# Moving the one other stage of a step ahead of the values on TensorE, in an attention and feed-forward kernel

## The chip, the cores and the metric

The kernel runs on one core of a Trainium2 chip. The metric is the device time of one execution in microseconds (us). The median of three runs of the kernel before is 1005.7 us (1003.91 to 1006.5). TensorE, VectorE, ScalarE, GpSimd and SyncE are called PE, DVE, ACT, POOL and SP, as in the profile. All numbers of the computation are 32-bit floats.

## The reference, cut to what matters

Eight batches of 512 query rows and 1024 context rows, width 256, 16 heads of 16 columns. Each batch goes through cross-attention and then through a feed-forward part that works on 128 selected rows:

```python
x = x + xattn(layernorm(x), ctx, ctx, mask, w_q, w_k, w_v, w_o)
x = x + ffn(layernorm(x), w_router, W_qkv, W_out, g1, g2, W1, W2, W3)

def xattn(q, k, v, mask, ...):          # 16 heads of 16
    scores = (q @ w_q.T) . (k @ w_k.T) / sqrt(16)     # per head, 512 x 1024
    attention = softmax(where(mask, -1e9, scores))
    return (attention . (v @ w_v.T)) @ w_o.T

def ffn(x, ...):                         # 128 of 512 rows
    idx = top_k(x @ w_router, 128)
    x_sel = x[idx]
    h = rmsnorm(x_sel, g1)
    x_attn = causal_attention(h @ W_qkv.T) @ W_out.T
    h2 = rmsnorm(x_sel + x_attn, g2)
    x_ff = silu(h2 @ W1.T) * (h2 @ W2.T) @ W3.T
    out = x.at[idx].set(x_sel + x_attn + x_ff)
```

## The kernel before, in words

Each batch is worked in 32 steps: four groups of four heads, eight tiles of 128 keys in each. In step `s` PE computes the scores of step `s` (`pe_scores`, L412, four matmuls that each use 32 rows of the array) into two of three pairs of PSUM banks. ACT takes the exponential of each pair (`act_scores`, L449, line L454), and writes it to `probs`. PE multiplies `probs` of the step before with the values (`pe_values`, L429, line L443), and adds them up in `o_bank` over the eight steps of a group. So the order on PE is scores of step `s`, then values of step `s - 1`.

The softmax needs one more pass when a group is complete. The last values of a group (steps 7, 15, 23 and 31; PE issues them in the step after, so those of step 31 in step 0 of the next batch) release `o_ready`. `dve_norm` (L526) then transposes `o_bank`, takes reciprocals, multiplies, and after groups 1 and 3 transposes again. These are the stages `norm0` to `norm3` of DVE.

Everything else is cut into other stages, at most two in a step. Stages of kind P belong to the projections of the next batch (`K00` to `K11`, `V0` to `V3`, `xT0`, `xT1`, `Q0`, `Q1`; `pe_project`, L252). Stages of kind F belong to the feed-forward part of the batch before (`wo0` to `scat0`; `pe_ffn`, L285). In a step without such a stage only scores and values run; it is called a plain step here. All these stages write one PSUM bank, `m_bank`. PE takes it with `take_bank` (L247; L248 and L249 are a wait on `bank_free`), and the next stage can start only when ACT or DVE has read the result of the last one out and released the bank. The exception is `fs`, the scores of the small attention, which uses the pairs of the ring.

The order of the stages is written out by hand for each engine. `PE_SLOT` gives for PE the kind, the stage, its step, and a flag that is called `early` in the loop at L994. With `early` the stage is issued between the scores and the values of its step, without it behind the values. Batch 0 has its own table, `PE_SLOT_0`. Batch 7 has no stage of kind P. `ACT_SLOT` places the stages that ACT reads out, always after both exponentials of the step. `DVE_ORDER` is a list without steps: DVE takes its stages strictly one after the other and waits at each for its input. Part of that list, which matters for the order of work:

```python
("F", "rank0"), ("F", "rank1"), ("N", "norm0"), ("F", "rank2"), ("F", "rank3"), ("P", "xn"), ("F", "gather"),
...
("F", "wout"), ("P", "V3"), ("N", "norm2"), ("F", "u0"), ("F", "w0"), ("F", "u1"), ("F", "w1"), ("F", "down"),
```

Some stages of PE wait for more than the bank. `gather` waits for the selection matrix `sel` that DVE makes in `rank0` to `rank3`. `Q0` waits for both halves of `xn_t`, which ACT copies out after `xT0` and `xT1`. `u0` waits for `hid2_t`, which ACT copies out after `hid2T`. The bank of `u0` is released by DVE in stage `u0` (L692), which stands behind `norm2` in `DVE_ORDER`.

Of the kernel before, what the change touches and what calls it, by code (L numbers as in the profile page):

```python
# [5 lines left out]
P = 128  # L6
# [43 lines left out]


FS_STEP = 16
PE_SLOT = [("P", "K00", 0, False), ("P", "K01", 1, False), ("F", "wo0", 2, False), ("F", "wo1", 3, False),
           ("P", "V0", 4, True), ("P", "K10", 5, False), ("F", "spread", 6, False), ("P", "K11", 7, False),
           ("F", "gather", 10, False), ("F", "selT", 11, False), ("F", "hidT", 12, False), ("P", "V1", 13, True),
           ("P", "xT0", 13, False), ("F", "kq", 14, False), ("F", "v", 15, False), ("F", "fs", FS_STEP, False),
# [4 lines left out]
ACT_SLOT = [("P", "K00", 0), ("P", "K01", 1), ("P", "K10", 5), ("F", "spread", 6), ("P", "K11", 7), ("P", "differ", 9),  # L61
            ("F", "selT", 11), ("F", "hidT", 12), ("P", "xT0", 13), ("F", "v", 15), ("F", "fs", FS_STEP), ("P", "xT1", 16),
            ("F", "hid2T", 23), ("F", "u0", 24), ("F", "u1", 26)]
# [33 lines left out]
def program(nc, io, out):  # L97
    with ExitStack() as top:
# [669 lines left out]
        def slots(b, table):  # L768

            has = {"A": b > 0, "F": b > 0, "N": True, "P": b < B - 1, "I": True}  # L770
            return [e[1:] + (e[0],) for e in table if has[e[0]]]
# [5 lines left out]
        with ExitStack() as ctx:  # L777
# [191 lines left out]
            def _(pe):  # L969
# [20 lines left out]
                for b in range(B):  # L990
                    todo = slots(b, PE_SLOT if b > 0 else PE_SLOT_0)
                    if b == 1:
# [316 lines left out]
```

## Time and profile before

| | |
|---|---|
| median of three runs | 1005.7 us |
| profiled execution: time | 1004.58 us |
| its span, first to last instruction | 1002.9 us |
| granted TensorE clock, mean | 0.973 |
| PE busy | 909.9 us (91%) |
| ACT busy | 575.9 us (57%) |
| DVE busy | 340.6 us (34%) |
| POOL busy | 78.7 us (8%) |

A row of the timeline gives the start in us, the busy time of the merged instructions, the engine, the line, the operation, what it writes and reads, and the count. Behind it stands in brackets how long the engine was idle before it, and on what it waited; `PEq` and `DVEq` are the sequencers of PE and DVE, and L422 and L249 lines in the semaphore handling of the scores and of `take_bank`. Every matmul of 32-bit floats shows as two instructions. Starts are recorded; the ends of matmuls are modelled, so distances are best taken from start to start.

### The profile page before, as it was taken

Reading aid. Unit: us, or ns where it says so; the run is one execution under the profiler, and the core shown is the slowest. Engines: PE = TensorE matmul, PEld = TensorE weight load, DVE = VectorE, ACT = ScalarE, POOL = GpSimd, SP = SyncE. Lnnn points to the kernel's source line nnn. Section 1 sums busy time; section 2 is a strip of 40 time slices with the busy share of each in tenths; the row PEclk is TensorE's granted clock in tenths of the full one; section 3 lists DMA queues with packets and bytes.
Section 4 is the critical chain, followed back from the end, with each engine's and each line's share of the span. In section 5 each row is a group of like instructions: output and inputs, shape, how many; then the busy total and the mean of one; then the engine's idle time right before and its main releaser. Section 6 shows DMA issues by size and latency. Waiting matters only on the chain. (4 is left out here: it accounts for less than half of the span.)

```text
span 1002.9 us, 16672 instructions
## 1 busy us (share of the span) xinstructions
PE 909.9 (91%) x6019; PEld 375.4 (37%) x6019; DVE 340.6 (34%) x886; ACT 575.9 (57%) x653; POOL 78.7 (8%) x130
## 2 busy tenths in 40 slices
PE   4999999999999999999989999999999998998345
PEld 2323232444333533444334433434334432343234
DVE  2122136231543227241452316331362315222621
ACT  2566757665566556755566556656576666664010
POOL 4000100010100101110000101020000100100010
PEclk9999999999999999999999999999999999999577
DMA  4050200110020100210020100201001000000000
GB/s 162 24 192 1 69 2 23 48 43 22 2 69 2 43 22 4 66 43 23 1 69 1 43 22 1 70 3 41 22 11 39 1 22 1 23 2 22 0 1 24
DMA packets 23757, 31.93 MB, mean 32 GB/s; under 512 B 1103, under 2 KB 20857, under 8 KB 23673
## 3 DMA queue, kind: packets, MB, share of 16 engines
q1 hardware_dynamic: 23672, 30.81, 9.2%
q8 instruction: 52, 0.85, 0.4%
q14 instruction: 33, 0.26, 0.1%
HBM read 26.61 MB, written 4.19 MB: 31 GB/s over the span
## 5 line engine op out<-in xcount | busy, mean ns | idle before, releaser
L454 ACT ACTIVATE probs<-pair_bank 128x1024 f32<-128x1024 f32 x512 | 496.3, 1021 | 281.5 <-ACTq L453 281.5
L424 PE MATMUL pair_bank<-q_sb,k_sb 32*128 32x512 f32 x2048 | 293.5, 641 | 18.0 <-PEq L422 17.9
L443 PE MATMUL o_bank<-probs,va 128*32 128x512 f32 x2048 | 272.8, 605 | 1.1 <-ACT probs L454 1.1
L424 PEld LDWEIGHTS pair_bank<-q_sb,k_sb 32*128 32x128 f32 x2048 | 82.3, 183 | 134.7 <-issue 130.5
L443 PEld LDWEIGHTS o_bank<-probs,va 128*32 128x32 f32 x2048 | 40.4, 108 | 190.3 <-issue 126.9
L244 PE MATMUL m_bank<-wv_sb,ctx_in 128*128 128x256 f32 x256 | 64.3, 394 | 0.3
L532 DVE STREAM_TRANSPOSE o_blk<-o_bank 128x512 f32<-128x512 f32 x32 | 22.9, 717 | 116.1 <-DVEq L531 116.1
L244 PE MATMUL m_bank<-ctx_in,wk_sb 128*128 128x512 f32 x120 | 59.5, 618 | 0.0
L244 PEld LDWEIGHTS m_bank<-wv_sb,ctx_in 128*128 128x128 f32 x256 | 46.3, 190 | 31.3 <-issue 26.2
L244 PEld LDWEIGHTS m_bank<-hid_t,w 128*128 128x128 f32 x360 | 43.7, 196 | 24.3 <-issue 24.3
L573 DVE TENSOR_SCALAR va<-m_bank,valid 128x256 f32<-128x256 f32 x64 | 28.0, 479 | 72.0 <-DVEq L567 72.0
L244 PE MATMUL m_bank<-hid_t,w 128*128 128x128 f32 x360 | 49.3, 288 | 0.7 <-PEq L249 0.7
L585 DVE TENSOR_SCALAR q_sb<-m_bank,parity 128x512 f32<-128x512 f32 x30 | 21.1, 746 | 48.7 <-DVEq L583 48.7
L244 PEld LDWEIGHTS m_bank<-ctx_in,wk_sb 128*128 128x128 f32 x120 | 20.3, 189 | 39.5 <-issue 39.5
L462 ACT ACTIVATE k_sb<-m_bank 128x512 f32<-128x512 f32 x30 | 17.9, 597 | 29.3 <-ACTq L461 29.3
L602 DVE TENSOR_TENSOR x<-x,m_bank 128x512 f32<-128x512 f32 x14 | 9.6, 688 | 66.7 <-DVEq L601 66.7
L750 POOL TENSOR_SCALAR veps<-mv 128x4 f32<-128x4 f32 x8 | 1.9, 233 | 361.1 <-POOLq L749 361.1
L244 PE MATMUL m_bank<-xn_t,wq_sb 128*128 128x512 f32 x60 | 29.8, 618 | 0.0
L628 DVE SCALAR_TENSOR_TENSOR ties<-all_scores,score,before 128x512 f32<-128x512 f32 x32 | 24.1, 752 | 14.8 <-DVEq L627 13.0
L757 POOL TENSOR_SCALAR_AFFINE_SELECT p_f<-p_f 128x2048 f32<-128x2048 f32 x8 | 16.0, 2004 | 153.2 <-POOLq L755 153.2
L244 PE MATMUL m_bank<-wo,o_t 128*128 128x256 f32 x112 | 27.9, 392 | 0.0
L742 POOL TENSOR_TENSOR mask_in<-mask_in,mask_row 128x256 int32<-128x256 int32 x32 | 23.3, 759 | 54.1 <-POOLq L739 54.1
(164 smaller groups left out, 652.0 us busy)
## 6 DMA issues: line engine op xcount, KB each, us to landing
ctx_in<-in_ctxT SPq DMA_DIRECT2D x8, 1024.0 KB, 5.0
x_in<-in_x SPq DMA_DIRECT2D x8, 512.0 KB, 4.0
x<-in_x SPq DMA_DIRECT2D x8, 512.0 KB, 3.8
mask_in<-in_mask SPq DMA_DIRECT2D x8, 512.0 KB, 4.7
out_dram<-out_sb SPq DMA_DIRECT2D x8, 512.0 KB, 2.8
mask_row<-in_mask SPq DMA_DIRECT2D x8, 128.0 KB, 4.7
wqkv<-in_wqkvT SPq DMA_DIRECT2D x1, 768.0 KB
w<-in_w1T SPq DMA_DIRECT2D x1, 682.0 KB
```

Of the source, the lines that this page charges most:

```text
L244: last = nc.tensor.matmul(dst, a, c, start=(n == 0), stop=(n == len(pairs) - 1))
L424: last = nc.tensor.matmul(pair_bank[pairs[r // 2]][:, r % 2], key_tile(b, s, r), query_tile(b, s, r), start=True, stop=True)
L443: last = nc.tensor.matmul(o_bank[32 * r:32 * r + 32], va[b % 2][:, t, HV * h:HV * h + 32], probs[s % 2][:, r], start=(t == 0), stop=(t == ...
L454: nc.scalar.activation(probs[s % 2][:, 2 * e:2 * e + 2, :], pair_bank[p][:], ACT.Exp, scale=HD ** -0.5).then_inc(s_free[p], 1)
L462: nc.scalar.activation(k_sb[b % 2][:, m, half * 512:(half + 1) * 512], bank[i], ACT.Copy).then_inc(bank_free[i], 1)
L532: nc.vector.transpose(o_blk[:], o_bank[:]).then_inc(o_free, 1)
L573: last = nc.vector.tensor_scalar(by_head(va[b % 2][:, t])[:, :, 0:HD], bank[i][:, e * D:(e + 1) * D].rearrange("p (h d) -> p h d", h=H), o ...
L585: last = nc.vector.tensor_scalar(q_sb[b % 2][:, m, par], bank[i], parity[:, par:par + 1], None, ALU.mult)
L602: nc.vector.tensor_tensor(x1[:, 2 * pr:2 * pr + 2], x1[:, 2 * pr:2 * pr + 2], bank[i].rearrange("p (t d) -> p t d", t=2), ALU.add).then_in ...
L628: nc.vector.scalar_tensor_tensor(out=ties[t % 2][:], in0=all_scores[:], scalar=score[:, t:t + 1], in1=before[:, t], op0=ALU.is_equal, op1= ...
L742: last = nc.gpsimd.tensor_tensor(mask_words[:, t * WORDS:(t + 1) * WORDS], mask_words[:, t * WORDS:(t + 1) * WORDS], first, ALU.subtract)
L757: nc.gpsimd.affine_select(out=flat, in_=flat, compare_op=ALU.is_ge, fill=0.0, base=0, pattern=[[0, H], [1, CAP]], channel_multiplier=-1).t ...
```

## The change

In `PE_SLOT` the flag `early` becomes true for every stage that is alone in its step. It was true for `V0` (step 4) and `V1` (step 13) already. `xT0` (the second stage of step 13) and `fs` and `xT1` (both of step 16) stay behind the values. Steps, `ACT_SLOT`, `DVE_ORDER`, and the table of batch 0 are as before.

```diff
-PE_SLOT = [("P", "K00", 0, False), ("P", "K01", 1, False), ("F", "wo0", 2, False), ("F", "wo1", 3, False),
-           ("P", "V0", 4, True), ("P", "K10", 5, False), ("F", "spread", 6, False), ("P", "K11", 7, False),
-           ("F", "gather", 10, False), ("F", "selT", 11, False), ("F", "hidT", 12, False), ("P", "V1", 13, True),
-           ("P", "xT0", 13, False), ("F", "kq", 14, False), ("F", "v", 15, False), ("F", "fs", FS_STEP, False),
-           ("P", "xT1", 16, False), ("P", "Q0", 17, False), ("P", "V2", 18, False), ("F", "pv", 19, False),
-           ("P", "Q1", 20, False), ("F", "wout", 21, False), ("P", "V3", 22, False), ("F", "hid2T", 23, False),
-           ("F", "u0", 24, False), ("F", "w0", 25, False), ("F", "u1", 26, False), ("F", "w1", 27, False),
-           ("F", "down", 28, False), ("F", "scat1", 29, False), ("F", "scat0", 30, False)]
+PE_SLOT = [("P", "K00", 0, True), ("P", "K01", 1, True), ("F", "wo0", 2, True), ("F", "wo1", 3, True),
+           ("P", "V0", 4, True), ("P", "K10", 5, True), ("F", "spread", 6, True), ("P", "K11", 7, True),
+           ("F", "gather", 10, True), ("F", "selT", 11, True), ("F", "hidT", 12, True), ("P", "V1", 13, True),
+           ("P", "xT0", 13, False), ("F", "kq", 14, True), ("F", "v", 15, True), ("F", "fs", FS_STEP, False),
+           ("P", "xT1", 16, False), ("P", "Q0", 17, True), ("P", "V2", 18, True), ("F", "pv", 19, True),
+           ("P", "Q1", 20, True), ("F", "wout", 21, True), ("P", "V3", 22, True), ("F", "hid2T", 23, True),
+           ("F", "u0", 24, True), ("F", "w0", 25, True), ("F", "u1", 26, True), ("F", "w1", 27, True),
+           ("F", "down", 28, True), ("F", "scat1", 29, True), ("F", "scat0", 30, True)]
```

The loop that reads the flag is unchanged (L994 to L1011).

## Rows read from the trace of the kernel before

**Rows 1.** The page: PE's busy time, and its costliest group.

```profile
PE 909.9 (91%) x6019; PEld 375.4 (37%) x6019; DVE 340.6 (34%) x886; ACT 575.9 (57%) x653; POOL 78.7 (8%) x130
...
L424 PE MATMUL pair_bank<-q_sb,k_sb 32*128 32x512 f32 x2048 | 293.5, 641 | 18.0 <-PEq L422 17.9
```

**Rows 2.** Timeline of PE, batch 2: step 4 (`V0` early), then steps 18, 19.

```profile
259.82 1.14 PE L424 MATMUL pair_bank<-q_sb,k_sb 32*128 32x512 f32 x8
260.89 1.99 PE L244 MATMUL m_bank<-wv_sb,ctx_in 128*128 128x256 f32 x8
262.82 1.07 PE L443 MATMUL o_bank<-probs,va 128*32 128x512 f32 x8
263.81 1.14 PE L424 MATMUL pair_bank<-q_sb,k_sb 32*128 32x512 f32 x8
...
310.57 1.14 PE L424 MATMUL pair_bank<-q_sb,k_sb 32*128 32x512 f32 x8
...
314.56 1.14 PE L424 MATMUL pair_bank<-q_sb,k_sb 32*128 32x512 f32 x8
```

**Rows 3.** Timeline of PE: `gather` of batch 2 and of batch 7.

```profile
282.68 1.97 PE L244 MATMUL m_bank<-y,sel 128*128 128x256 f32 x8 [1.26 <-PEq L249]
...
851.68 1.97 PE L244 MATMUL m_bank<-y,sel 128*128 128x256 f32 x8 [1.68 <-PEq L249]
```

**Rows 4.** Timeline of DVE and PE, batch 2: a bank is released by DVE, PE takes it.

```profile
292.97 0.88 DVE L573 TENSOR_SCALAR va<-m_bank,valid 128x256 f32<-128x256 f32 x2 [4.16 <-DVEq L567]
...
293.99 0.63 PE L239 MATMUL m_bank<-ident,xn 128*128 128x128 f32 x4 [0.18 <-PEq L249]
```

**Rows 5.** Timeline of the last part, ACT and PE: `hid_t` copied out, `kq` starts.

```profile
954.92 0.38 ACT L491 ACTIVATE hid_t<-m_bank 128x256 f32<-128x256 f32 x1 [2.10 <-ACTq L490]
...
955.63 3.27 PE L244 MATMUL pair_bank<-hid_t,wqkv 128*128 128x128 f32 x16 [0.84 <-PEq L249]
```

**Rows 6.** Timeline of PE, ACT and DVE, batch 3, steps 24 and 25.

```profile
446.80 0.39 ACT L503 ACTIVATE hid_t<-m_bank 128x256 f32<-128x256 f32 x1
447.22 1.07 PE L443 MATMUL o_bank<-probs,va 128*32 128x512 f32 x8
...
448.22 1.60 PE L244 MATMUL m_bank<-hid_t,w 128*128 128x128 f32 x12
448.47 0.72 DVE L532 STREAM_TRANSPOSE o_blk<-o_bank 128x512 f32<-128x512 f32 x1 [3.65 <-DVEq L531]
...
449.61 0.43 DVE L537 TENSOR_TENSOR o_nrm<-o_blk,inv_all 128x256 f32<-128x256 f32 x1
449.75 1.14 PE L424 MATMUL pair_bank<-q_sb,k_sb 32*128 32x512 f32 x8
```

**Rows 7.** Timeline of DVE, batch 2: stage `u0` right behind `norm2`.

```profile
335.57 0.56 DVE L692 SCALAR_TENSOR_TENSOR silu<-half_tanh,m_bank 128x384 f32<-128x384 f32 x1 [0.29 <-DVEq L691]
```

**Rows 8.** Timeline of PE and ACT, batch 2: step 17 and the copy of `xn_t`.

```profile
306.59 1.14 PE L424 MATMUL pair_bank<-q_sb,k_sb 32*128 32x512 f32 x8 [0.70 <-PEq L422]
307.56 0.60 ACT L469 ACTIVATE xn_t<-m_bank 128x512 f32<-128x512 f32 x1 [0.20 <-ACTq L468]
```

**Rows 9.** Timeline of PE and ACT, batch 2: step 7, and the copy of `all_scores`.

```profile
270.44 1.14 PE L424 MATMUL pair_bank<-q_sb,k_sb 32*128 32x512 f32 x8
270.88 0.60 ACT L481 ACTIVATE all_scores<-m_bank 128x512 f32<-128x512 f32 x1
```

**Rows 10.** Timeline of DVE, batch 2: reading out `V0`.

```profile
263.66 0.87 DVE L573 TENSOR_SCALAR va<-m_bank,valid 128x256 f32<-128x256 f32 x2
```

**Rows 11.** Timeline of PE at the start of the kernel.

```profile
22.98 0.25 PE L975 MATMUL pair_bank<-ident,rows 64*128 64x64 f32 x1 [2.17 <-PEq L249]
...
27.78 1.99 PE L244 MATMUL m_bank<-wv_sb,ctx_in 128*128 128x256 f32 x8
```

**Rows 12.** Windows: length, busy time (instructions) of PE, PEld, DVE, ACT, POOL, granted clock, DMA.

```profile
24.50:25.00 0.50, 0.50 (x3) 0.41 (x2) 0.00 (x0) 0.00 (x0) 0.00 (x0) 0.50 0.00 0
...
853.00:916.00 63.00, 59.76 (x468) 24.24 (x466) 14.29 (x31) 41.74 (x47) 3.47 (x5) 1.00 0.03 10
```

## The prediction, made before the changed kernel ran

> **What bounds the kernel now.** I read the page first, then PE's rows in the timeline of one batch, then ACT and DVE beside them. The page has PE busy for 909.9 us of the span; its scores waited 18.0 us in all for a free pair [rows 1], and its values next to nothing. So inside the batches PE is the bound, and ACT and DVE matter only where PE meets a semaphore. The change takes no instruction away. It can gain only from waits that exist (the 18.0 us are nearly all behind plain steps, which it doesn't touch), and lose by waits that it makes.
>
> **The order itself.** The trace has both forms. Step 4 holds `V0` early: scores to stage 1.07, stage to values 1.93, values to next scores 0.99, together 3.99 us. Step 18 holds `V2`, the same work, behind the values: 314.56 - 310.57 = 3.99 us [rows 2]. I take 0 for the order. The bounds are the rounding of such distances, 0.02 us either way, and 174 moved stages (26 in each of batches 1 to 6, 18 in batch 7): -3.5 to +3.5 us.
>
> **What moves in time.** A moved stage starts 1.0 us earlier in its step, and the values in that step start later by the stage's length. Between two moved stages nothing changes: all distances on PE are kept, and so is the time for reading `m_bank` out, if the reader is not held up by something tied to the scores or the values. ACT's copies are tied to the scores, because they stand behind the exponentials. DVE's norms are tied to the values. SP's transfers depend on releases that move by 1 us and are needed much later: nothing. What stands behind a waiting stage on PE is now the values too, so a wait no longer has them as cover. The places where that matters:
>
> *gather, step 10.* `sel` ends a chain (scores of step 6, copy of `all_scores` on ACT, four ranks with `norm0` between them) that hangs on scores and on the values of a plain step, so it comes no earlier. PE already idles 1.26 us before `gather` [rows 3], with the values of step 9 done ahead of it. Now these stand behind `gather`: the wait becomes 1.26 + 0.99 = 2.25 us and the step 0.99 us longer [rows 2, 3]. Seven batches.
>
> *w0, step 25.* The largest term. The bank of `u0` is released by DVE behind `norm2`, and `norm2` waits for the values of step 23, which now stand behind `u0`. Take batch 3 [rows 6], with the scores of step 24 at 446.15 (447.22 - 1.07): `u0` wants to start at 447.22, where the values stood. Its input is copied out by 446.80 + 0.39 = 447.19. From a copy's end over ACT's drain to PE takes 955.63 - 955.30 = 0.33 [rows 5], so `u0` starts at 447.52: a wait of 0.30. The values follow after 449.75 - 448.22 = 1.53, at 449.05, the scores of step 25 after 0.99 at 450.04, and `w0` wants to start at 451.11. `norm2` starts 448.47 - 447.22 = 1.25 after its values, at 450.30, and ends 450.04 - 448.47 = 1.57 later, at 451.87. Stage `u0` on DVE begins 0.29 after that and takes 0.56 [rows 7], to 452.72; a bank released by DVE is taken by PE 293.99 - 293.85 = 0.14 later [rows 4], so `w0` starts at 452.86: a wait of 1.75. With the 0.30 this is 2.05 us in each of seven batches. Before, `norm2` was over ahead of the tanh and cost nothing.
>
> *Q0, step 17.* `xT1` stays behind the values of step 16, `Q0` moves ahead. `xn_t` is ready at 307.56 + 0.60 + 0.33 = 308.49, `Q0` wants to start at 306.59 + 1.07 = 307.66 [rows 5, 8]: 0.83 us in six batches. The values of step 16 used to cover this.
>
> *K11, step 7.* `all_scores` is copied behind the exponentials until 271.48, the bank is free at 271.62, `K11` wants to start at 270.44 + 1.07 = 271.51 [rows 4, 9]: 0.11 us. `hidT` in step 12 meets the same copy behind a short stage, 0.11 us; in batches 1 to 6 the small wait that `V1` has today takes it up, in batch 7 nothing does.
>
> *Close, but covered.* `K10` after the early `V0`: DVE has read `V0` out by 264.53, the bank is free at 264.67, `K10` wants 263.81 + 1.07 = 264.88 [rows 4, 10]; 0.2 us of cover, and each tenth lost beyond would cost 0.6 us over six batches. `norm3` waits for values now behind `K00` (1.9 us later), and `wo0` needs its result two steps on, over 2 us after it is done by the durations of [rows 6]. The other moved stages keep their distance of a whole step of 3 to 4 us to a reader that needs about 2.
>
> Sum of the waits: 6 x (0.99 + 2.05 + 0.83 + 0.11) = 23.9, and 0.99 + 2.05 + 0.11 = 3.1 for batch 7: 27.0 us. The bounds of the unseen parts: 21 (if DVE's `u0` follows `norm2` by a tenth, and drains cost half) to 31 (if each hand-off is 0.1 us longer).
>
> **The clock.** The longest idle time of PE inside the batches is 1.68 us, and there the granted clock stays 1.00 behind it [rows 3, 12]. At the start of the kernel PE idles 2.17 us, does 0.2 us of work and goes on, and the clock then is at 0.50, 1.2 GHz, from about 24.3 [rows 11, 12]. The price: from 22.98 to 27.78 are 4.80 us, for 0.18 + 1.93 + 1.07 = 3.18 us of work at 2.4 GHz [rows 2, 11]: 1.6 us. The new idle time before `gather`, 2.25 us (2.67 in batch 7), is nearest to the 2.17 us after which it fell, but one case doesn't say that it always falls; the 1.7 us before `w0` is nearest to the case that kept it. Bounds 0 to 7 falls, 0 to 11.4 us; I take three, 4.9 us.
>
> The Trainium skill (TensorE: Matmul & The Clock Gate, section Why this matters for your kernels) asks that idle gaps between bursts of matmuls be kept short, and its limit is longer than each gap forecast here. By it there is no fall, and the time is that of the first rival. The 2.17 us of [rows 11] speak against it.
>
> **Forecast.** The profiled execution took 1004.6 us (span 1002.9). 1004.6 + 27.0 + 4.9 = 1036.5; the median of the runs is 1.1 above that execution, so 1037 us, 3.1% slower. Chance 0.46, with its own range of 1031 to 1042.
>
> **Rivals.** *The clock holds.* All waits come as summed, the idle time before `gather` leaves the clock at 2.4 GHz: 1004.6 + 27.0, about 1032. For it speaks that PE works densely on both sides of the gap. 0.22.
>
> *The clock falls every time.* At all seven gathers, 11.4 us, and perhaps at some `w0`: 1043 to 1050. 0.12.
>
> *Half is absorbed.* If DVE's `norm2` is not what holds `w0` (say `u0` gets its bank back at the old distance), 7 x 1.75 = 12.3 go and 1019 to 1024 remain. `DVE_ORDER` speaks against it, since DVE can't pass a waiting stage. 0.13.
>
> *Faster.* One mechanism: ACT finds the result of the moved stage ready when its exponentials end, copies at once, and starts the next exponentials earlier, so PE's waits for free pairs go. These are 18.0 us in all [rows 1]; if the 0.70 us of step 17 [rows 8] and half of the others went and the new waits did not come, the time would be 1004.6 - 9 = 996. It decides where a copy delays an exponential by more than PE's slack. Against it: in the steps with copies PE doesn't wait for pairs. 0.03. No change within the measurement, because the 3.99 us are all that counts: 0.04.
>
> A measurement of this kernel tells 0.3%, 3 us, from no change. Faster 0.03, same 0.04, slower 0.93. The range takes in the forecast, the held clock, and part of each side case: 1023 to 1045.
>
> **What would show it.** In the profile after: `gather` with 2.2 to 2.7 us idle before it, seven times; `w0` with 1.7 us and DVE's silu right behind the multiplication of `norm2`; `Q0` with 0.8 us; `u0` with 0.3 us; PE busy still near 910 us if the clock holds, 5 to 12 us more if it falls, with windows below 1.00 behind `gather`. Scores wait as before, 18 us. The prediction is wrong if `w0` has no wait, if moved steps without a wait differ from 3.99 us, or if the scores' waits shrink.

## The result: 3.1% slower, 1035.7 us

| | before | changed |
|---|---|---|
| median | 1005.0 us (4 runs) | 1035.7 us (4 runs, 1033.42 to 1046.1) |
| profiled execution | 1004.58 us, span 1002.9 | 1037.44 us, span 1035.7 |
| PE busy | 909.9 us | 916.4 us |
| granted clock, mean | 0.973 | 0.966 |

The medians are 3.1% apart (the forecast was 1037 us). Over all runs the ratio is 1.0326, with a 95% interval of 1.0271 to 1.0381. The four runs of the changed kernel differ more than those of before, and the longer they are the lower is their mean clock: 0.971 at 1033.42 us, 0.966 at 1037.44, 0.956 at 1046.1.

PE does the same work and is 6.5 us longer busy with it. Nearly all of the rest of the 32.8 us is waiting. The page after, against [rows 1]:

```profile
PE 916.4 (88%) x6019; PEld 378.7 (37%) x6019; DVE 340.6 (33%) x886; ACT 573.7 (55%) x653; POOL 78.7 (8%) x130
...
L424 PE MATMUL pair_bank<-q_sb,k_sb 32*128 32x512 f32 x2048 | 292.4, 639 | 18.1 <-PEq L422 17.9
```

The scores wait as long for pairs as before, 17.9 us. What is new shows in PE's waits for `m_bank` (columns: who waited for whom, us in total, times, longest). Line L244 had 10.1 us in 8 waits before.

```profile
PE m_bank L244 <- PEq L249: 35.5, 29, 2.6
```

The timeline of PE after, `gather` of batches 2, 3 and 7, answers to [rows 3]. The idle time grew from 1.26 to 2.25 us, and the values of step 9 now stand behind it (288.50). In batch 3 the clock fell there: `gather` took 2.68 us instead of 1.97, and the values behind it 1.87 us to the next start instead of 0.99.

```profile
286.61 1.97 PE L244 MATMUL m_bank<-y,sel 128*128 128x256 f32 x8 [2.25 <-PEq L249]
288.50 1.07 PE L443 MATMUL o_bank<-probs,va 128*32 128x512 f32 x8
289.50 1.14 PE L424 MATMUL pair_bank<-q_sb,k_sb 32*128 32x512 f32 x8
...
407.39 2.68 PE L244 MATMUL m_bank<-y,sel 128*128 128x256 f32 x8 [2.26 <-PEq L249]
410.00 1.94 PE L443 MATMUL o_bank<-probs,va 128*32 128x512 f32 x8
411.87 1.14 PE L424 MATMUL pair_bank<-q_sb,k_sb 32*128 32x512 f32 x8
...
881.32 1.97 PE L244 MATMUL m_bank<-y,sel 128*128 128x256 f32 x8 [2.60 <-PEq L249]
```

Steps 24 and 25 of batch 3 after, all engines, answer to [rows 6]. Read it as a chain: `hid_t` copied (ACT L503), `u0` 0.23 us late, the values of step 23 behind it (462.09), `norm2` on DVE (463.34), then stage `u0` on DVE (465.11), then `w0` (465.81) after 1.57 us of idle time. The tanh had been ready since 462.87.

```profile
459.21 1.14 PE L424 MATMUL pair_bank<-q_sb,k_sb 32*128 32x512 f32 x8
459.87 0.39 ACT L503 ACTIVATE hid_t<-m_bank 128x256 f32<-128x256 f32 x1
460.59 1.58 PE L244 MATMUL m_bank<-hid_t,w 128*128 128x128 f32 x12 [0.23 <-PEq L249]
462.09 1.07 PE L443 MATMUL o_bank<-probs,va 128*32 128x512 f32 x8
462.38 0.49 ACT L512 ACTIVATE half_tanh<-m_bank 128x384 f32<-128x384 f32 x1
463.09 1.14 PE L424 MATMUL pair_bank<-q_sb,k_sb 32*128 32x512 f32 x8
463.34 0.72 DVE L532 STREAM_TRANSPOSE o_blk<-o_bank 128x512 f32<-128x512 f32 x1 [6.46 <-DVEq L531]
...
464.49 0.43 DVE L537 TENSOR_TENSOR o_nrm<-o_blk,inv_all 128x256 f32<-128x256 f32 x1
465.11 0.55 DVE L692 SCALAR_TENSOR_TENSOR silu<-half_tanh,m_bank 128x384 f32<-128x384 f32 x1 [0.19 <-DVEq L691]
465.81 1.57 PE L244 MATMUL m_bank<-hid_t,w 128*128 128x128 f32 x12 [1.57 <-PEq L249]
```

`Q0` and `K11` of batch 2, PE's timeline, answer to [rows 8, 9]: `K11` starts 275.48 - 274.29 = 1.19 us after the scores instead of 1.07, `Q0` waits 0.76 us.

```profile
274.29 1.14 PE L424 MATMUL pair_bank<-q_sb,k_sb 32*128 32x512 f32 x8
275.48 1.96 PE L244 MATMUL m_bank<-ctx_in,wk_sb 128*128 128x512 f32 x4
...
313.41 1.96 PE L244 MATMUL m_bank<-xn_t,wq_sb 128*128 128x512 f32 x4 [0.76 <-PEq L249]
```

The granted clock in windows of the profile after (columns as in [rows 12]): 1.00 behind `gather` of batch 2, 0.50 behind that of batch 3 and behind `w0` of batch 2.

```profile
286.60:290.00 3.40, 3.39 (x20) 1.89 (x24) 2.20 (x7) 0.54 (x1) 0.09 (x1) 1.00 0.14 28
...
345.00:347.00 2.00, 2.00 (x12) 1.50 (x15) 0.25 (x1) 0.00 (x0) 0.00 (x0) 0.50 0.00 0
408.50:410.00 1.50, 1.50 (x4) 0.69 (x3) 0.23 (x1) 0.00 (x0) 0.00 (x0) 0.50 0.01 4
```

The length of each batch, from its first scores to those of the next (batch 7: to the last values), read from PE's timeline of each profile, holds the whole account. A star marks a fall of the clock in the batch. The labels are those of the experiments below; "undisturbed" means without a star and without the 0.35 us of batches 2, 4 and 6 that are explained later.

| us | 1 | 2 | 3 | 4 | 5 | 6 | 7 |
|---|---|---|---|---|---|---|---|
| before | 115.11 | 115.11 | 115.11 | 115.62 | 115.11 | 115.12 | 100.61 |
| changed | 118.87 | 120.78* | 120.55* | 120.92* | 118.87 | 120.81* | 103.34 |
| e1, four stages | 120.47* | 120.79* | 120.38* | 120.76* | 118.79 | 120.66* | 104.63* |
| e2, norm2 later | 117.26 | 118.89* | 119.00* | 117.62 | 118.89* | 118.89* | 101.74 |
| e3, the rest | 115.36 | 115.37 | 115.37 | 115.72 | 115.37 | 115.37 | 100.47 |
| e4, four more matmuls | 120.02 | 121.93* | 120.02 | 120.37 | 120.02 | 120.36 | 104.14 |
| e6, two more matmuls | 118.73 | 119.07 | 118.73 | 119.08 | 118.81 | 120.63* | 104.45* |
| e8, u0 and w0 | 117.01 | 117.35 | 116.99 | 117.50 | 116.99 | 118.95* | 102.34 |
| e5, V1 | 114.28 | 114.04 | 114.06 | 114.04 | 114.11 | 114.06 | 100.60 |
| e7, V1 and v | 113.80 | 113.57 | 113.57 | 113.84 | 113.64 | 113.56 | 100.19 |

### The profile page after: what moved, and what is told of

It is laid out like the page before. It is cut to its first block and busy times, and to the rows that moved or that the text cites. A ratio compares the mean times of both kernels' runs of the same rounds, so it can differ in the third digit from the quotient of the medians.

```text
span 1035.7 us, 16672 instructions
## 1 busy us (share of the span) xinstructions
PE 916.4 (88%) x6019; PEld 378.7 (37%) x6019; DVE 340.6 (33%) x886; ACT 573.7 (55%) x653; POOL 78.7 (8%) x130
## 5 line engine op out<-in xcount | busy, mean ns | idle before, releaser
L424 PE MATMUL pair_bank<-q_sb,k_sb 32*128 32x512 f32 x2048 | 292.4, 639 | 18.1 <-PEq L422 17.9
L244 PE MATMUL m_bank<-wv_sb,ctx_in 128*128 128x256 f32 x256 | 65.2, 399 | 0.7 <-PEq L249 0.7
L244 PE MATMUL m_bank<-hid_t,w 128*128 128x128 f32 x360 | 51.5, 297 | 14.1 <-PEq L249 14.1
L244 PE MATMUL m_bank<-ctx_in,wk_sb 128*128 128x512 f32 x120 | 59.3, 617 | 0.3
L244 PEld LDWEIGHTS m_bank<-hid_t,w 128*128 128x128 f32 x360 | 46.0, 205 | 35.9 <-issue 35.9
L244 PEld LDWEIGHTS m_bank<-wv_sb,ctx_in 128*128 128x128 f32 x256 | 46.9, 193 | 30.1 <-issue 24.7
L244 PEld LDWEIGHTS m_bank<-ctx_in,wk_sb 128*128 128x128 f32 x120 | 20.3, 189 | 38.1 <-issue 38.1
L244 PE MATMUL m_bank<-xn_t,wq_sb 128*128 128x512 f32 x60 | 29.6, 615 | 4.6 <-PEq L249 4.6
L244 PE MATMUL m_bank<-y,sel 128*128 128x256 f32 x56 | 16.2, 439 | 16.2 <-PEq L249 16.2
L244 PE MATMUL m_bank<-wo,o_t 128*128 128x256 f32 x112 | 27.9, 392 | 0.0
```

The lines of the kernel that those rows point to most:

```text
L244: last = nc.tensor.matmul(dst, a, c, start=(n == 0), stop=(n == len(pairs) - 1))
L424: last = nc.tensor.matmul(pair_bank[pairs[r // 2]][:, r % 2], key_tile(b, s, r), query_tile(b, s, r), start=True, stop=True)
```

## The experiments

My theory: the loss is the waits of `gather`, `u0`, `w0` and `Q0`, which used to lie under the values or did not exist, and the falls of the clock in the idle time that they leave. Rivals: that the order scores, stage, values costs a little everywhere, that something else than `norm2` holds `w0`, and that the falls have another cause.

### Four stages alone

```diff
-("F", "gather", 10, False) ... ("P", "Q0", 17, False) ... ("F", "u0", 24, False), ("F", "w0", 25, False)
+("F", "gather", 10, True) ... ("P", "Q0", 17, True) ... ("F", "u0", 24, True), ("F", "w0", 25, True)
```

(In the kernel before.)

> The kernel before, with only four stages of PE_SLOT made early: gather, Q0, u0 and w0 (27 of the 174 moved stages). Theory (four places make the loss, the other stages cost nothing): gather +0.99 and u0/w0 +0.30 and +1.64 us in seven batches, Q0 +0.83 in six: +25.5 us, and a few falls of the clock at 1.6 us each, so 1031 to 1037 us, with the same idle time before the four stages as in the changed kernel (2.25, 1.57, 0.76, 0.23 us). Rival (the order scores, stage, values itself costs a little in each of the 174 moved stages): 27 of 174 of the loss, about 1010 us.

Measured: 1038.4 us median of 4 runs, ratio to before 1.0316 (1.0289 to 1.0344). PE's timeline has the same waits as the changed kernel, `gather` and `Q0` of batch 2 and `w0` of batch 3:

```profile
287.96 1.97 PE L244 MATMUL m_bank<-y,sel 128*128 128x256 f32 x8 [2.25 <-PEq L249]
...
314.76 1.95 PE L244 MATMUL m_bank<-xn_t,wq_sb 128*128 128x512 f32 x4 [0.76 <-PEq L249]
...
467.08 1.57 PE L244 MATMUL m_bank<-hid_t,w 128*128 128x128 f32 x12 [1.57 <-PEq L249]
```

27 of the 174 moved stages bring nearly the whole loss: the one undisturbed batch takes 118.79 us, which is 3.68 of the 3.76 us that a batch of the changed kernel has over before. The median is 1 us above my range: this profile has six falls in the batches, not "a few". The rival of a price on each stage, 1010 us, is out.

### The other stages alone

```diff
-("F", "gather", 10, True), ("P", "Q0", 17, True), ("P", "V2", 18, True), ("F", "u0", 24, True), ("F", "w0", 25, True)
+("F", "gather", 10, False), ("P", "Q0", 17, False), ("P", "V2", 18, False), ("F", "u0", 24, False), ("F", "w0", 25, False)
```

(In the changed kernel.)

> The changed kernel, with gather, Q0, u0, w0 and V2 behind the values again (V2 because it stands one step behind Q0 and would wait for its bank). 141 stages stay moved. Theory: only small waits stay, K11 0.12 us in six batches, hidT 0.1, and pv about 0.2 us in six batches, since it follows a V2 that is late: +2 us, 1006 to 1008 us, no fall of the clock inside the batches. Rival (each moved stage costs a little): 141 of 174 of the loss, about 1030 us.

Measured: 1006.8 us (10 runs), before 1005.1 (15 runs), ratio 1.0014 (1.0005 to 1.0024). A batch takes 0.26 us more: 0.09 in the step of `K11` and 0.17 in that of `pv`. No fall of the clock inside the batches. The waits for `m_bank` on L244 are back at the size of before:

```profile
PE m_bank L244 <- PEq L249: 9.9, 8, 1.6
```

So 141 stages between scores and values cost about 1.6 us together, and those two waits are nearly all of it. The order itself costs nothing here.

### norm2 behind u0 on DVE

```diff
-("N", "norm2"), ("F", "u0"), ("F", "w0"),
+("F", "u0"), ("N", "norm2"), ("F", "w0"),
```

(In `DVE_ORDER` of the changed kernel.)

> The changed kernel, with one entry moved in DVE_ORDER: norm2 behind u0 instead of ahead of it; PE's order is untouched. Theory (DVE's list holds the bank of u0 behind norm2): the idle time before w0 goes from 1.57 us (1.92 in two batches) to 0, 12 us in all, and with it the falls of the clock that came there, 0 to 5 us; 1019 to 1024 us. The 0.23 us before u0, 0.76 before Q0 and 2.25 before gather stay. Rival (the copy of the tanh on ACT or the drain of the array holds w0): the wait stays, 1034 to 1037 us.

Measured: 1027.4 us (5 runs), ratio to before 1.0218 (1.0197 to 1.0239), 8.3 us less than the changed kernel. DVE's and PE's timelines, batch 3: DVE reads out `u0` first (460.09), `w0` starts right behind the scores (461.23) and waits for nothing, while `u0` keeps its 0.23 us.

```profile
460.09 0.55 DVE L692 SCALAR_TENSOR_TENSOR silu<-half_tanh,m_bank 128x384 f32<-128x384 f32 x1 [6.14 <-DVEq L691]
460.95 0.72 DVE L532 STREAM_TRANSPOSE o_blk<-o_bank 128x512 f32<-128x512 f32 x1 [0.30 <-DVEq L531]
```

```profile
457.66 1.58 PE L244 MATMUL m_bank<-hid_t,w 128*128 128x128 f32 x12 [0.23 <-PEq L249]
...
460.16 1.14 PE L424 MATMUL pair_bank<-q_sb,k_sb 32*128 32x512 f32 x8
461.23 1.60 PE L244 MATMUL m_bank<-hid_t,w 128*128 128x128 f32 x12
```

An undisturbed batch is 118.87 - 117.26 = 1.61 us shorter: `norm2` in front of the read-out is the cause. The median is 3 us above my range. Falls are why: I took those at `w0` away and forgot that those at `gather` vary; this profile has four there, the one of the changed kernel two. Another 1.6 us lie behind the last values (1026.0 - 941.65 = 84.3 us, against 82.7), in a part that this edit doesn't touch. There PE does the same 186 instructions in 37.31 us instead of 35.79, so this is the clock too (windows of this kernel, then of the changed one). Why it was low for longer there stays open.

```profile
941.65:1026.00 84.35, 37.31 (x186) 28.99 (x186) 29.02 (x78) 6.25 (x11) 4.75 (x7) 0.66 0.02 7
952.99:1035.70 82.71, 35.79 (x186) 28.07 (x186) 29.05 (x78) 6.24 (x11) 4.75 (x7) 0.67 0.02 7
```

### u0 and w0 alone

```diff
-("F", "u0", 24, False), ("F", "w0", 25, False)
+("F", "u0", 24, True), ("F", "w0", 25, True)
```

(In the kernel before.)

> The kernel before, with only u0 and w0 early. Theory (norm2 in front of stage u0 on DVE, plus the copy of hid2_t): idle 0.23 to 0.3 us before u0 and 1.57 us before w0 in seven batches, a batch 115.1 + 1.9 = 117.0 us, falls of the clock at most in the two batches with 1.92 us of idle time: 1018 to 1022 us. Rival (the loss at w0 needs the other moved stages, since they shift what DVE has to do): under 1012 us.

Measured: 1020.4 us (4 runs), ratio 1.0145 (1.0128 to 1.0162), as the theory had it. The pair needs no other moved stage. Its timeline of PE shows `w0` of batches 2, 3 and 6, and with them that the same idle time doesn't always bring a fall: 1.93 us and no fall (339.62), 1.92 us and a fall, 2.65 us for the same work (808.46).

```profile
339.62 1.58 PE L244 MATMUL m_bank<-hid_t,w 128*128 128x128 f32 x12 [1.93 <-PEq L249]
456.61 1.58 PE L244 MATMUL m_bank<-hid_t,w 128*128 128x128 f32 x12 [1.57 <-PEq L249]
...
808.46 2.65 PE L244 MATMUL m_bank<-hid_t,w 128*128 128x128 f32 x12 [1.92 <-PEq L249]
```

### The idle time before gather filled

```diff
+dst = take_bank(pe, i)
+for n in range(4):
+    nc.tensor.matmul(dst, ident[:], y[:, 0:2], start=(n == 0), stop=(n == 3))
 pe.wait_ge(sel_ready, 1)
 pe.sem_inc(sel_ready, -1)
-dst = take_bank(pe, i)
```

(In the changed kernel, stage `gather`.)

> The changed kernel, with four more matmuls of 128x512 in the stage gather, ahead of its wait for sel, into the bank that gather then overwrites. They are extra work whose result is not used. Theory (the idle time before gather makes the clock fall in some batches, at 1.6 us a fall): 1.9 of the 2.25 us of idle time are filled, gather starts at the same time, the clock stays 1.00 behind every gather, and the runs lie at 1030 to 1034 us with a mean clock of 0.970 or more, against 1033 to 1046 us and 0.956 to 0.971 of the changed kernel. Rival (the falls don't come from that gap): the spread of times and clocks stays as it was, and there are windows below 1.00 behind gather.

Measured: 1038.0 us (5 runs, 1035.93 to 1040.35), clocks 0.972 to 0.978. The time was mis-forecast by a plain error of size: I counted 0.47 us a matmul, and each is two instructions of 0.44. The four took 3.53 us and pushed `gather` back:

```profile
285.14 3.70 PE L304 MATMUL m_bank<-y,ident 128*128 128x512 f32 x8
288.67 1.89 PE L244 MATMUL m_bank<-y,sel 128*128 128x256 f32 x8
```

In this profile the clock did what the theory says (no fall behind any `gather`, one behind `w0` of batch 2); the time can't be compared. So once more with two:

```diff
-for n in range(4):
-    nc.tensor.matmul(dst, ident[:], y[:, 0:2], start=(n == 0), stop=(n == 3))
+for n in range(2):
+    nc.tensor.matmul(dst, ident[:], y[:, 0:2], start=(n == 0), stop=(n == 1))
```

> As the filled kernel of the first round, but with two more matmuls of 128x512 instead of four. There each took 0.88 us, so the four lasted 3.53 us and held gather back by 1.2 us in each batch; two last 1.8 us and fit into the 2.25 us of idle time. They are extra work whose result is not used. Theory (the idle time before gather lets the clock fall): a batch takes 118.9 us as in the undisturbed batches of the changed kernel, no fall behind gather, at most one in the two batches where w0 waits 1.92 us: 1031 to 1034 us, spread under 4 us, against 1033 to 1046 us of the changed kernel. Rival: falls and spread as before, 1034 to 1046 us.

Measured: 1031.7 us (5 runs, 1029.92 to 1033.44), clocks 0.971 or 0.972 in all five. By the medians the changed kernel with more work is 4 us faster than without; the two intervals just touch (1.0257, up to 1.0273, against 1.0326, from 1.0271). PE's timeline, `gather` of batch 2 and `w0` of batch 6, where a fall remained:

```profile
283.74 1.98 PE L304 MATMUL m_bank<-y,ident 128*128 128x512 f32 x4
285.91 1.97 PE L244 MATMUL m_bank<-y,sel 128*128 128x256 f32 x8 [0.19 <-PEq L306]
...
818.70 2.25 PE L244 MATMUL m_bank<-hid_t,w 128*128 128x128 f32 x12 [1.92 <-PEq L249]
```

There is no fall behind any of the seven `gather`. Not all of the 4 us is the clock. The edit also takes the bank ahead of the wait for `sel`, and an undisturbed batch is 118.87 - 118.73 = 0.14 us shorter, 1 us in all. The traces show where: `gather` starts 0.17 us after the end of DVE's last write of `sel` (285.74), in the changed kernel 0.32 (286.29 to 286.61). Taking the bank first, without the extra matmuls, was not tested. The second fall of this profile I hadn't expected: in batch 7 behind the 1.28 us before the scores of step 17, an idle time that the kernel before has too.

### Two versions that use the reading

The same account (PE is the bound, a wait is worth what it lasts, an idle gap is filled by a stage from a double step) gives a better table. First `V1` out of the double step 13 into the plain step 8 (cut to what changes):

```diff
-("P", "V1", 13, True), ("P", "xT0", 13, False)                   # PE_SLOT
+("P", "V1", 8, False), ... ("P", "xT0", 13, False)
-("F", "rank2"), ("F", "rank3"), ..., ("P", "V1"), ("F", "kq")   # DVE_ORDER
+("F", "rank2"), ("P", "V1"), ("F", "rank3"), ..., ("F", "kq")
```

> The kernel before, with V1 moved from step 13 (where it shares the step with xT0) to step 8, behind the values, and in DVE_ORDER between rank2 and rank3. Nothing else changes. Theory (PE is the bound and its waits are worth what they last): step 8 gets 1.56 us longer, since V1's 1.92 us cover the 0.36 us that a plain step waits; gather moves 1.2 us later, its 1.26 us of idle time shrink to about 0.9; step 13 loses 1.92 us and the waits around V1 and xT0 of 0.12 and 0.18 us: -1.0 us in each of six batches, 999 us. Rival (the rank chain on DVE, now with V1 in it, sets gather and grows by more than PE gains): no gain or a loss, 1005 to 1008 us.

Measured: 998.5 us (6 runs), ratio to before 0.9932 (0.992 to 0.9944). PE's timeline, batch 2: `V1` covers the wait of step 9, `gather` waits 0.87 us instead of 1.26. An ordinary batch takes 1.05 us less (115.11 to 114.06).

```profile
275.11 1.99 PE L244 MATMUL m_bank<-wv_sb,ctx_in 128*128 128x256 f32 x8
277.03 1.14 PE L424 MATMUL pair_bank<-q_sb,k_sb 32*128 32x512 f32 x8
...
282.47 1.97 PE L244 MATMUL m_bank<-y,sel 128*128 128x256 f32 x8 [0.87 <-PEq L249]
```

Then, on top of it, `v` beside `fs` in place of `xT1`:

```diff
-("F", "kq", 14, False), ("F", "v", 15, False), ("F", "fs", 16, False), ("P", "xT1", 16, False)
+("P", "xT1", 14, False), ("F", "kq", 15, False), ("F", "fs", 16, False), ("F", "v", 16, False)
```

(`ACT_SLOT` likewise.)

> The kernel with V1 in step 8, and in addition xT1 in step 14, kq in step 15 and v in step 16 behind fs (before: kq 14, v 15, xT1 16). Theory: v (1.06 us) covers more than xT1 (0.59 us) of the wait for the exponential of fs, 0.70 us before the scores of step 17: -0.47 us in six batches, and -0.7 us in batch 7, where v leaves a step of its own: 995 to 996 us. Rival (kq one step later is too late for fs): fs waits and the gain goes, 999 us or more.

Measured: 994.9 us (5 runs), ratio to before 0.9898 (0.9884 to 0.9911), the fastest of all kernels here. Batch 7 gains 0.41 us, not 0.7; its step 17 is 0.31 us longer than before. The wait of the scores of step 17 went from 0.70 to 0.22 us:

```profile
299.99 1.15 PE L407 MATMUL pair_bank<-q_f,k_f 32*128 32x256 f32 x16 [0.30 <-PEq L403]
301.06 1.13 PE L244 MATMUL m_bank<-wqkv,hid_t 128*128 128x256 f32 x4
302.42 1.14 PE L424 MATMUL pair_bank<-q_sb,k_sb 32*128 32x512 f32 x8 [0.22 <-PEq L422]
```

## Why the prediction was right, step by step

**The order is free.** Forecast 0, with bounds of 3.5 us. Shown by the 141 stages of e3: 1.6 us, nearly all of it the waits of `K11` and `pv`. It also shows in a moved step without a wait. PE's timeline after, step 18 of batch 2 with `V2` now early, takes 320.28 - 316.29 = 3.99 us, as before [rows 2]:

```profile
316.29 1.14 PE L424 MATMUL pair_bank<-q_sb,k_sb 32*128 32x512 f32 x8
317.36 1.99 PE L244 MATMUL m_bank<-wv_sb,ctx_in 128*128 128x256 f32 x8
319.28 1.07 PE L443 MATMUL o_bank<-probs,va 128*32 128x512 f32 x8
320.28 1.14 PE L424 MATMUL pair_bank<-q_sb,k_sb 32*128 32x512 f32 x8
```

**gather.** Forecast 2.25 us idle and 0.99 us lost; measured 2.25, and 289.50 - 286.61 = 2.89 us from `gather` to the next scores, against 1.90.

**u0 and w0.** Forecast 0.30 and 1.75 us. Measured, with the modelled 0.07 us end of a matmul added to the idle times, 0.30 and 1.64: DVE began to read out 0.19 us behind `norm2`, not 0.29. I had taken the gap from the one row where it stood, [rows 7], in another context. The cause was tested by itself: `norm2` behind `u0`, and 1.61 us a batch are gone.

**Q0 and K11.** Forecast 0.83 and 0.11; measured 0.76 + 0.07 and 0.12. `Q0` was not tested by itself.

**The sum of the waits.** Forecast 3.98 us a batch and 3.1 in batch 7, together 27.0. Measured on undisturbed batches 118.87 - 115.11 = 3.76, and 103.34 - 100.61 = 2.73, together 25.3. The named waits add up to 3.88; stages that had to wait run 0.03 us shorter (1.50 us from `u0` to the next start, not 1.53), which four times is the other 0.12. In batch 7 `u0` costs 0.11 us only, because before the scores ahead of it took 892.85 - 891.62 = 1.23 us to the values there, not 1.07.

**A term I missed, 0.7 us.** In batches 2 and 6 `norm2` is over 0.35 us later than in the others, for two reasons that the trace of before has as well. In batch 2 it starts later (DVE idle 4.00 us before it, 3.65 in batch 3). In batch 6 it starts on time and idles 0.43 us between the reciprocal and the multiplication. DVE's timeline after, batches 2 and 6:

```profile
341.24 0.72 DVE L532 STREAM_TRANSPOSE o_blk<-o_bank 128x512 f32<-128x512 f32 x1 [6.81 <-DVEq L531]
...
823.50 0.43 DVE L537 TENSOR_TENSOR o_nrm<-o_blk,inv_all 128x256 f32<-128x256 f32 x1 [0.43 <-issue]
```

Nothing waited for this before. Now it goes straight into `w0`: 1.92 us of idle time instead of 1.57. Why DVE is late there is not known. (Batch 4 is 0.35 us longer in its step 13, with the change and without.)

**The clock.** Forecast three falls at 1.6 us, all at `gather`. The profile has four, 6.4 us in all: the step of the fall is 1.56, 1.59, 1.69 and 1.59 us longer than the same step without one (batches 2, 3, 4 and 6). Size and number were about right, the places half: two at `gather`, two at those `w0` with 1.92 us, where I had expected the clock to hold. Together 25.3 + 0.7 + 6.4 = 32.4 us in the batches, and 0.4 behind the last values: the 32.8 us of the spans. My 31.9 came near by luck: the waits were 1.7 too large and the rest 2.2 too small. One sum is also off: 1036.5 + 1.1 is 1037.6, not 1037.

**The rivals.** *The clock holds* was not seen. Without its four falls the profiled execution would have taken 1037.4 - 6.4 = 1031.0 us, an estimate, where I had 1032; the kernel with the idle time filled comes near it with 1031.7 us, but has two falls and the shorter hand-off to `gather`. The limit on idle gaps in the Trainium skill (TensorE: Matmul & The Clock Gate, section Why this matters for your kernels) would have given no fall in the batches of the changed kernel; the clock fell at gaps of 2.26 and 1.92 us, so here the measurement decides against it. *Falls every time* was not seen in a profile, but the run of 1046.1 us, with a mean clock of 0.956, is in its range. *Half is absorbed* and *faster* failed at the same rows: `w0` waits, and the scores' waits are 17.9 us as before. The price of *faster* was itself too small: it takes the 0.70 us of step 17 once, but they stand in each of batches 1 to 6, and 1.28 us in batch 7. With them the time would have been 993 us, not 996.

## What to carry to other kernels

Here, moving a stage in the queue that is the bound cost nothing by itself; look for what it was issued behind. A wait that used to have work ahead of it in its queue is longer by that work, and work that is now behind it is late for whoever waits for it in an ordered list on another engine (here DVE's `norm2`, and through it the bank of `u0`). Before changing an order, write down for each moved stage its release and what that release hangs on: those tied to a neighbour that also moves can be skipped, the others are the whole account.

## What the runs showed of the hardware that was not expected

The clock falls after short idle times, and not always after the same. Over the ten profiles: never after the 1.57 us before `w0` (25 cases), in 6 of 10 cases after 1.92 us at the same place, in 10 of 21 after 2.25 to 2.67 us before `gather`, in none of 14 once that gap was filled, and in 2 of 9 cases in batch 7 after 1.28 us that had 0.30 us of idle time and 1.15 us of `fs` ahead of it. The 2.17 us at the start of the kernel [rows 11] stand in all ten profiles with the same instructions around them. The clock falls behind them in nine; in e7 it stays at 1.00, and the scores start 24.62 - 22.69 = 1.93 us after `V0`, not 25.76 - 23.16 = 2.60 as before. So the length of one gap doesn't decide alone. Each fall inside the batches costs 1.5 to 1.7 us of a queue that is the bound (about 1.3 for the two in batch 7), and makes the times of one kernel differ from run to run: 13 us over four runs of the changed kernel, 4 us over five once the gap was filled with work for nothing. What else decides, was not tested.
